# Routed experts on one Trainium2 core: tiles of two 64-row halves, each half with its own expert, on two column tiles of TensorE

## The reference, cut to what matters

```
scores = sigmoid(x @ gate_w)
_, selected = top_k(scores + expert_bias, 2)
shared = silu(x @ shared_gate_w) * (x @ shared_up_w) @ shared_down_w
for e in range(16):                      # widths: x 512, gu 512, hidden 256, out 512
    g, u = split(x @ experts_gate_up[e], 2)
    routed += comb[:, e:e+1] * (silu(g) * u @ experts_down[e])
return shared + routed
```

## Time and profile before

| | before |
|---|---|
| median of 3 runs | 1167.46 us (1167.3 to 1170.01) |
| the profiled execution's own time | 1169.68 us |
| its span, first to last instruction | 1167.9 us |
| TensorE busy | 1109.7 us, 95% |
| VectorE busy | 778.0 us, 67% |
| ScalarE busy | 596.6 us, 51% |
| GpSimd busy | 511.3 us, 44% |
| mean granted TensorE clock | 0.994 |

### The profile page before, as it was taken

How to read it: one execution, slowest core, us unless ns; L and a number is a source line. 1 busy time by engine, 2 the same in 40 slices (tenths; PEclk the granted TensorE clock), 3 DMA queues, 4 the chain that set the end, 5 groups by cost and what they waited for, 6 DMA issues and landing times. The chain is left out here.

```text
span 1167.9 us, 28720 instructions
## 1 busy us (share of the span) xinstructions
PE 1109.7 (95%) x11466; PEld 669.1 (57%) x11468; DVE 778.0 (67%) x1325; ACT 596.6 (51%) x945; POOL 511.3 (44%) x597
## 2 busy tenths in 40 slices
PE   6979999899999999899999999999999999999996
PEld 5757755445566544566555555556544555555554
DVE  6636768757897665669675787987658455555453
ACT  6635554535665453666544466666632444444443
POOL 6567544324443331354232122110102477777776
PEclk9989999999999999999999999999999999999999
DMA  6333853303471321166330234220225776788640
GB/s 142 105 112 93 187 140 116 67 3 97 91 148 39 123 52 31 42 120 119 91 88 16 70 85 93 84 35 3 76 91 159 206 195 120 171 244 246 187 85 9
DMA packets 119596, 122.07 MB, mean 105 GB/s; under 512 B 25472, under 2 KB 84992, under 8 KB 119344
## 3 DMA queue, kind: packets, MB, share of 16 engines
q1 hardware_dynamic: 101744, 98.59, 32.0%
q0 software_dynamic: 17008, 21.16, 9.6%
q10 hardware_dynamic: 720, 0.61, 0.2%
HBM read 94.63 MB, written 40.77 MB: 116 GB/s over the span
## 5 line engine op out<-in xcount | busy, mean ns | idle before, releaser
L898 DVE TENSOR_REDUCE mx<-ps_m 128x2 f32<-128x1024 f32 x176 | 214.8, 1221 | 147.1 <-PE ps_m L1337 74.9
L1165 ACT ACTIVATE prob<-ps_s 128x1024 f32<-128x1024 f32 x164 | 168.1, 1025 | 214.4 <-PE ps_s L1335 111.0
L2284 PE MATMUL ps_gu<-ring,xgT 128*128 x376 | 176.9, 593 | 1.5 <-DVE xgT L1959 1.0
L1894 POOL DMA_INDIRECT out<-y,dest x92 | 146.6, 1594 | 60.6 <-issue 32.0
L594 POOL TENSOR_TENSOR pieces<-wring,pieces 128x512 fp32r<-128x512 f32 x88 | 116.5, 1329 | 64.8 <-ACT pieces L1134 63.4
L1343 PE MATMUL acc<-xnT_high,pieces 128*128 128x512 f32 x256 | 139.7, 546 | 4.0 <-POOL pieces L594 2.3
L1579 PE MATMUL ps_o<-prob,values 128*32 128x128 f32 x4096 | 139.5, 274 | 0.0
L1579 PEld LDWEIGHTS ps_o<-prob,values 128*32 128x32 f32 x4096 | 113.0, 109 | 36.3 <-issue 32.0
L1161 ACT ACTIVATE prob<-ps_s 128x512 f32<-128x512 f32 x184 | 99.8, 595 | 63.1 <-PE ps_s L1337 62.8
L894 DVE TENSOR_REDUCE mx<-ps_m 128x1 f32<-128x512 f32 x160 | 102.5, 681 | 21.9 <-PE ps_m L1337 21.3
L1337 PE MATMUL ps_s<-q_stack,k_stack 99*32 99x512 bf16 x1296 | 104.1, 380 | 2.7 <-ACT prob L1165 2.7
(11 more groups left out here) (354 smaller groups left out, 2007.0 us busy)
## 6 DMA issues: line engine op xcount, KB each, us to landing
ring<-in_w_experts SPq DMA_DIRECT2D x96, 256.0 KB
wring<-in_w_in SPq DMA_DIRECT2D x80, 256.0 KB, 3.4
q_stack<-part_rows SPq DMA_DIRECT2D x96, 128.0 KB, 4.7
wring<-in_w_out SPq DMA_DIRECT2D x32, 256.0 KB, 3.3
part_rows<-part SPq DMA_DIRECT2D x20, 384.0 KB, 4.1
out<-x SPq DMA_DIRECT2D x4, 1024.0 KB, 5.4
xt<-in_x SPq DMA_DIRECT2D x14, 256.0 KB, 3.5
k_stack<-part_rows SPq DMA_DIRECT2D x48, 64.0 KB, 2.7
```

Source lines behind the costliest of these rows:

```text
L898: nc.vector.tensor_reduce(mx[:, n % G, 2 * u:2 * u + 2], ps_m[:, :, :], AX.X, ALU.max).then_inc(s_max, 2)
L1165: nc.scalar.activation(prob[:, slot % PROB, :, :], ps_s[:, :, :], ACT.Exp, scale=SCALE).then_inc(s_exp, 2)
L1894: pool.indirect_dma_start(out=out[:, :], out_offset=bass.IndirectOffsetOnAxis(ap=dest[:, k, n:n + 1], axis=0), in_=y[:, n % YB, :], in_off ...
L2284: ins = nc.tensor.matmul(ps_gu[p][:, :], xgT[:, p, k * P:(k + 1) * P], weights(own)[:, k * 2 * F:(k + 1) * 2 * F], start=(k == 0), stop=(k ...
```

## The change

A tile is still 128 places, but made of two halves of 64 that may have an expert each. The experts' tokens are filled up to 64 instead of 128 places, so that 40 tiles do in place of 47 (`TILES`); with these counts 73 halves hold tokens. Only the last expert begins at a whole tile. The table has two rows now: partition 0 of `own_i` tells of a tile's first half, partition 64 of its second.

Each product with expert weights becomes two matmuls of 64 stationary columns, one at column tile (0, 0) with the weights in `ring` and one at (0, 64) with those in a fixed buffer `second`. ScalarE copies the gate and up weights of the second half's expert there, in two pieces of 128 x 1024, and VectorE the down weights, for every tile. The splitting in high and low parts is gone: down is plain float32 as gate_up is, 4 matmuls of 64 columns in place of 6 of 128. TensorE's order is another too: both transposes now stand together, between the halves of gate_up, and down comes after gate_up. SyncE waits for each load to land before it goes on to the next. GpSimd adds a tile's high rows two tiles later, not one.

```diff
-    TILES = (TOP * TOKENS - E) // P + E
+    ROWS = P // 2
+    TILES = ((TOP * TOKENS - E) // ROWS + E + 2) // 2
...
+        second = nc.alloc_sbuf_tensor_at("second", [P, WCOLS], F32, offset=nc.sbuf_base - WCOLS * 4)
...
                 load(e)
-                if e > RING:
-                    ready(e - 1)
-            ready(E - 1)
+                ready(e)
...
             for n in range(TILES):
                 if n >= 2:
-                    add_high(n - 1)
+                    add_high(n - 2)
                 if n < TILES - 1:
                     add_low(n)
...
+            add_high(TILES - 2)
             add_high(TILES - 1)
...
+            last_start = bounds[:, E - 1:E]
+            V.then(nc.vector.tensor_scalar(whole[:, :], last_start, float(ROWS), None, ALU.add))
+            V.then(nc.vector.tensor_scalar(whole[:, :], whole[:, :], -P, None, ALU.bitwise_and))
+            V.then(nc.vector.tensor_copy(last_start, whole[:, :]))
...
-            nc.vector.tensor_copy(ends_i[:, :], ends[0:1, :]).then_inc(s["table"], 1)
+            V.then(nc.vector.tensor_scalar(ends_i[:, :], ends[0:1, :], 1.0, None, ALU.add))
+            nc.vector.tensor_scalar(ends_i[:, :], ends_i[:, :], 1, None, ALU.logical_shift_right).then_inc(s["table"], 1)
...
+            def copy_down(n):
+                slot_n = second_slot(mybir.EngineType.DVE, n)
+                dve.wait_ge(s["gu"], n + 1)
+                at_least(dve, s["dn"], n)
+                nc.vector.tensor_copy(second[:, WUP:WCOLS], in_slot(slot_n, WUP, WCOLS)).then_inc(s["second_down"], 1)
...
             for n in range(TILES):
+                if n:
+                    copy_h(n - 1, (n - 1) % 2)
                 if n + 1 < TILES:
                     copy_x(n + 1, (n + 1) % 2)
                 gated(n, n % 2)
                 if n + 1 < TILES:
                     weigh(n + 1)
-                if n:
-                    low_weights(n)
-                low_h(n, n % 2)
+                copy_down(n)
+            copy_h(TILES - 1, (TILES - 1) % 2)
...
+            def copy_gate_up(n, last, own):
+                half = slice(WUP // 2 * last, WUP // 2 * (last + 1))
+                if last:
+                    at_least(act, s["gu"], n)
+                else:
+                    act.wait_ge(s["wready"], own[0])
+                    at_least(act, s["gu_first"], n)
+                nc.scalar.activation(second[:, half], in_slot(own[1], half.start, half.stop), ACT.Copy
+                                     ).then_inc(s[("second_first", "second_last")[last]], 1)
...
-            for n in range(1, TILES):
-                high_h(n - 1, (n - 1) % 2)
+            for n in range(TILES):
+                if n + 1 < TILES:
+                    own = second_owner(n + 1)
+                    copy_gate_up(n + 1, 0, own)
                 silu(n, n % 2)
-                high_weights(n)
-                copy_y(n - 1, (n - 1) % 2)
+                if n + 1 < TILES:
+                    copy_gate_up(n + 1, 1, own)
+                if n:
+                    copy_y(n - 1, (n - 1) % 2)
...
+            def two_products(dst, stationary, own, first, last, start, stop):
+                nc.tensor.matmul(dst[0:ROWS, :], stationary[:, 0:ROWS], in_slot(own[1], first, last), start=start,
+                                 stop=stop, tile_position=(0, 0))
+                return nc.tensor.matmul(dst[ROWS:P, :], stationary[:, ROWS:P], second[:, first:last], start=start,
+                                        stop=stop, tile_position=(0, ROWS))
...
-                own = owners(n + 1, count)
+                own = owners(n - 1, count + 1)
                 for m in range(count):
+                    p = (first + m) % 2
                     more, q = divmod(first + m + 1, XG)
-                    step(n + m, (first + m) % 2, own[m], q, lap + more)
+                    gate_up(n + m, p, own[m + 1], turned_h=(n + m - 1, 1 - p),
+                            turned_x=None if last and m == count - 1 else (n + m + 1, 1 - p, q, lap + more))
+                    down(n + m - 1, 1 - p, own[m])
+                return own[count]
```

More of the change, by code:

```diff
@@ L1760, in experts_phase @@
         ends_i = sb("ends_i", [1, E], mybir.dt.int32)
-        owner_i = sb("owner_i", [1, TILES], mybir.dt.int32)
-        own_i = sb("own_i", [1, TILES, 2], mybir.dt.int32)
+        owner_i = sb("owner_i", [P, TILES], mybir.dt.int32)
+        own_i = sb("own_i", [P, TILES, 2], mybir.dt.int32)
+        side = sb("side", [P, 1])
+        whole = sb("whole", [P, 1], mybir.dt.int32)
+        turns = sb("turns", [P, TILES])
         hS = sb("hS", [P, KF, 512])
@@ L1993, in _ @@
             V.then(nc.vector.tensor_copy(iota_h[:, :], iota[:, :]))
+            V.then(nc.vector.tensor_scalar(side[:, :], column[:, :], float(ROWS), None, ALU.is_gt))
+            V.then(nc.vector.tensor_scalar(turns[:, :], iota[:, 0:TILES], 2.0, side[:, 0:1], ALU.mult, ALU.add))
             V.then(nc.vector.tensor_scalar(names[:, :], first_row[:, :], column[:, 0:1], None, ALU.add))
@@ L2262, in owners, with gate_up @@
                                                       "is masked with RING - 1")
[L2263 to L2264 removed]
+                _, slots_of = nc.values_load_multi_w_load_instructions(
+                    own_i[0:1, bass.ds(n, count), 1:2].rearrange("p g w -> p (g w)"), max_val=RING - 1, **one_engine)
+                _, loaded = nc.values_load_multi_w_load_instructions(
+                    own_i[ROWS:ROWS + 1, bass.ds(n, count), 0:1].rearrange("p g w -> p (g w)"), max_val=E, **one_engine)
                 in_ring = lambda a: nc.s_assert_within(a, 0, RING - 1, skip_runtime_bounds_check_because=(
                     "the table holds it masked with RING - 1"))
[L2267 to L2272, removed]
+                return [(loaded[m], in_ring(slots_of[m])) for m in range(count)]
+            def two_products(dst, stationary, own, first, last, start, stop):
[3 more added lines that the diff above has]
+                                        stop=stop, tile_position=(0, ROWS))
+            def gate_up(n, p, own, turned_h=None, turned_x=None):
                 pe.wait_ge(s["wready"], own[0])
@@ L2278, in gate_up @@
                     pe.wait_ge(s["sacc"], 4)
+                pe.wait_ge(s["second_first"], n + 1)
                 for k in range(KD):
-                    if between is not None and k == KD // 2:
-                        transpose_h(*between)
-                    if second is not None and k == KD // 2:
-                        transpose_x(*second)
-                    ins = nc.tensor.matmul(ps_gu[p][:, :], xgT[:, p, k * P:(k + 1) * P],
-                                           weights(own)[:, k * 2 * F:(k + 1) * 2 * F],
-                                           start=(k == 0), stop=(k == KD - 1))
+                    if k == KD // 2:
+                        if turned_h is not None:
+                            transpose_h(*turned_h)
+                        if turned_x is not None:
+                            transpose_x(*turned_x)
+                        pe.wait_ge(s["second_last"], n + 1)
+                    ins = two_products(ps_gu[p], xgT[:, p, k * P:(k + 1) * P], own, k * 2 * F, (k + 1) * 2 * F,
+                                       start=(k == 0), stop=(k == KD - 1))
+                    if k == KD // 2 - 1:
+                        ins.then_inc(s["gu_first"], 1)
                 ins.then_inc(s["gu"], 1)
@@ L2323, in _ @@
             pe.wait_ge(s["sacc"], 1)
-            own = owners(0, 2)
-            gate_up(0, 0, own[0], second=(1, 1, 1, 0))
-            gate_up(1, 1, own[1], between=(0, 0))
+            gate_up(0, 0, owners(0, 1)[0], turned_x=(1, 1, 1, 0))
             steps(1, 2, 1)
-            with pe.Fori(0, (TILES - 5) // STEP) as i:
+            with pe.Fori(0, (TILES - 4) // STEP) as i:
                 steps(STEP * i + 3, STEP, 3, i)
-            steps(TILES - 2, 1, (TILES - 2) % XG, (TILES - 2) // XG)
-            down(TILES - 2, 1)
-            transpose_h(TILES - 1, 0)
-            down(TILES - 1, 0)
+            own = steps(TILES - 1, 1, (TILES - 1) % XG, (TILES - 1) // XG, last=True)
+            transpose_h(TILES - 1, (TILES - 1) % 2)
+            down(TILES - 1, (TILES - 1) % 2, own)
 def build(nc, dram, out):
```

103 lines of the change are left out of this document (42 added, 61 removed).

## The result

The kernel became slower, not faster. The median of 5 runs is 1173.95 us (1171.41 to 1178.58) against 1167.89 (1167.3 to 1170.01) for the kernel before on the same chip: a ratio of 1.0044, 95% interval 1.0028 to 1.006. Forecast were 1155.4 us, and the range ended at 1168. The profiled execution took 1171.41 us, its span is 1169.6; it is the fastest of the five.

A forecast was written before the change was run, and what follows sets the result against it. The prediction took TensorE's work per tile to bound the expert stage. Its terms, -15.6 + 1.0 + 1.1 + 0 + 1.4 = -12.1 us, took the 1167.46 base to 1155.4 us, range 1144 to 1168.

The forecast's parts named there:

- The loop's top: Six times TensorE's queue takes the branch and two register loads before gate_up: plus 1.0 us, bounds nothing and 0.5 each pass.
- the tile: TensorE's work per tile in the expert stage: 6.07 us against 5.467, with 40 tiles for 47; minus 15.6 us.
- its pieces 0.86 and 0.92: Within a tile on TensorE: 0.86 us for a pair of 64-column matmuls, 0.92 for the block of six transposes.
- the cost of changing mode: TensorE's array going from column tiles to whole and back once a tile: about 0.27 us.
- the bound below: Lower bound for the six-transpose block if changes of mode are free: 0.58 us (0.36 + 0.22).
- VectorE's copy: Copy of the second half's down weights, between 0.6 and 1.2 us a tile, hidden behind TensorE and costing nothing.
- Expert 12: Its weight load, issued after load 11 lands, is tight at tile 28: plus 1.1 us, bounds 0 and 7.
- The tail: From the last gate_up to the span's end: 17.5 us against 16.05, so plus 1.4.
- Passes that queue: Rival: strict matmul order delays second columns, 0.43 us a tile, +17.2, so 1172.6 us, beat 6.5; chance 0.12.
- Serial column tiles: Rival: column tiles of 64 don't run side by side, pairs take 1.72 us, adding 206, so 1361; chance 0.03.
- Late weights: Rival: loads taking 12 us make the tight place cost 7 rather than 1.1, so 1161 us; chance 0.12.
- Changes of mode are not free: Judges the rival that changes of mode are free: 0.34 us a tile goes, 13.6, so 1141.8; chance 0.08.

The follow-up runs named there:

- The experiment with two loads side by side: Changed kernel keeping both register loads, table laid out so that each load's seven values are adjacent, not 8 bytes apart: 1169.33 us, ratio 0.9997.
- the one moved by 8 bytes: Against the kernel with two loads of adjacent values: table two columns wider, first load's values 16 bytes later, second's 8 bytes later: 1166.65 us in one run.
- the first experiment: Changed kernel with TensorE's second register load at the loop's top and its wait on `wready` taken out: 1159.04 us, ratio 0.9909.
- the two kernels with one load: Changed kernel without the second register load and its wait: 1159.04 us; the same with the load's values side by side: 1158.88 us.
- with expert 12 too: Kernel with one load of values side by side, SyncE issuing expert 12's load before waiting for expert 11's to land: 1157.11 us, ratio 0.9895.
- the experiment without column tiles: Kernel with one load of values side by side, each pair made one 128-column matmul with the first half's weights, second expert left out: 1150.66 us, ratio 0.9847.

## Why the prediction was wrong

**The step that failed** is the term "The loop's top", "two register loads, not one, of 0.85 each", "Plus 1.0 (0.16 each), nearer to nothing", with bounds of nothing and 0.5 a pass. It measured 16.8, 2.8 a pass, outside its bounds. The runs showed in its place two loads of 1.9 to 2.6 us each, one after the other, with 2.6 us of cover for both. Three things in it were wrong.
- The price. 0.85 was the duration of one form, twelve numbers side by side, used for another, seven numbers two apart, which takes 1.9 in the median, up to 2.6. The view gave a duration for a load, not for this load; the bound above should have been open. The experiment with two loads side by side and the one moved by 8 bytes show that layout and place change it, and the kernel before with two strided loads shows a load of six at 1.5 without the rest of the change.
- The cover. I set "Down, with 1.72 of work, and half of gate_up before it" against the loads, 3.4 us, but the queue comes to the loads only 2.6 us before down ends; in the kernel before, with other loads, 3.0. Two loads of 0.85 with the 0.5 around them, 2.2 by estimate, would still have been hidden, so this matters only with the price.
- What a gap brings with it. After two of the six gaps the clock is halved for 3.4 us, 1.6 to 1.7 each, some 3.3 of the 16.8. The prediction had no such term. It may be part of why these runs scatter: of the five, the slowest (1178.58 and 1176.12) have a mean clock of 0.988 and the fastest 0.991.

The size of the loss is shown by the first experiment: without the second load and its wait it goes, all of it. That the wait isn't what counts is shown by the short tops of the kernel with both loads side by side, which keep it.

**Right:** the tile (6.07 forecast, 6.11 found), with its pieces 0.86 and 0.92 (0.91), and the cost of changing mode, 0.27 forecast and 0.26 to 0.3 found. (That the 0.92 fits rests on the price of four transposes alone too, 0.43 and not the 0.36 seen in a row: without changes of mode the block of six takes 0.65, and not the 0.58 of the bound below.) VectorE's copy took 0.69 at the median, within its bounds, and no engine but TensorE set the beat. Expert 12 is the one tight place; its 1.1 was 0.4 in the change, 1.0 and 1.7 in the two kernels with one load. The tail was 18.4 against 17.5: the last addition started 12.9 after the last gate_up (12.8 forecast), and the end came 5.5 after it, not 4.7.

With the loads mended, the two kernels with one load take 1159, and 1157.1 with expert 12 too, near the 1155.4 that were forecast for this change. Against the kernel before on their chips they are 10.5, 10.7 and 11.7 us shorter, where 12.1 were forecast.

**The rivals.** Passes that queue gave 1172.6, and the measured time lies close to it; but the mechanism is refuted, since second columns start 0.01 us after the first and the beat is not 6.5. The right time for the wrong reason would have passed for a proof, had only the total been looked at. The Trainium skill, TensorE: Matmul & The Clock Gate, section The mechanism, has matmuls in strict order; the order of starts agrees, and that a second pass of one matmul keeps back the first of the next on another column tile is not seen here, with pairs 0.86 long. Serial column tiles (1361) are refuted by the same rows. Late weights cost 0.4 us at the one tight place, and not 7. Changes of mode are not free, as the experiment without column tiles shows.

## What to carry to other kernels

A register load at a loop's top is priced by its form: how many values, how far apart, and where they lie. If the trace has no load of that form, its price is open above, and it is cheaper not to load a register that serves only a wait which other waits cover. When engines show "issue" gaps at a fixed distance, look at the queue's own loads first; and a short gap on TensorE is not paid once, since the clock may fall behind it.

## What was not expected of the hardware

- Register loads by TensorE's queue in the loop: twelve numbers side by side 0.85 us, six two apart 1.4 to 1.9, seven two apart 1.8 to 2.6, seven side by side 1.1 to 1.6 where they start at a multiple of 16 bytes from the table's start and 1.7 to 2.6 where they start 8 bytes behind one. The count of registers alone does not set it. The Trainium skill, Runtime: NRT & Kernel Launch, section Instruction fetch mechanics, gives about 200 ns a register for such loads, which the page describes as loads from HBM; here, from on-chip memory, it is 71 ns each for twelve in one row and 270 for seven apart. Why the place matters is open, no other start was tried, and the end moved with it. Open too is why twelve take less than seven, and why the first of the loop's loads is the longest, 2.4 to 2.6, in each kernel that loads seven.
- The lower clock for 3.4 us behind gaps of 2.1 to 2.3 us, at two tops of six in the change and two of six in the kernel with both loads side by side, and once in the whole-array kernel, at a wait of 2.6. At the other tops it doesn't come, though their gaps are up to 2.2 as well. What picks them is open.
- A float32 pair of 64 columns on two column tiles takes what one matmul of 128 columns takes, 0.86, and going to the whole array and back costs 0.26 to 0.3 a time.
